# A four-batch, four-stage network on one core: the batch loop against four batches written out

## What is computed

```
x = u
x += gate * long_conv(mod(layernorm(x)))
x += gate * binary_ffn(mod(layernorm(x)))
x += gate * attention(mod(layernorm(x)))
x += gate * moe_top2(mod(layernorm(x)))
```

## Time and profile before

| | us |
|---|---|
| median of 3 executions | 2077.36 |
| lowest and highest | 2071.31, 2079.77 |
| the profiled execution's own time | 2071.98 |
| its span, first to last instruction | 2070.2 |
| around the span | 1.8 |
| mean granted clock of TensorE | 0.925 |
| busy: PE, DVE, ACT, POOL | 1795.0, 1520.4, 994.4, 735.9 |

### The profile page before, as it was taken

How to read it: one execution, slowest core, us unless ns; L and a number is a source line. 1 busy time by engine, 2 the same in 40 slices (tenths; PEclk the granted TensorE clock), 3 DMA queues, 4 the chain that set the end, 5 groups by cost and what they waited for, 6 DMA issues and landing times.

```text
span 2070.2 us, 27393 instructions
## 1 busy us (share of the span) xinstructions
PE 1795.0 (87%) x9108; PEld 1441.8 (70%) x9108; DVE 1520.4 (73%) x2758; ACT 994.4 (48%) x2129; POOL 735.9 (36%) x763
## 2 busy tenths in 40 slices
PE   6877789999875879999977779999987687999997
PEld 3755677777764757777765567777776575777786
DVE  4588878875659778887458887888564977788746
ACT  1313266777320347777431326677732033676743
POOL 0052245543225144454115224544321513455321
PEclk7888899999998989999989899999998897999998
DMA  6500244341410043543150024444141004344315
GB/s 231 203 1 1 77 123 119 98 104 42 188 53 1 1 122 98 139 118 73 29 223 0 1 62 135 112 107 103 43 187 54 1 1 122 98 118 123 78 27 203
DMA packets 92187, 187.17 MB, mean 90 GB/s; under 512 B 29119, under 2 KB 44287, under 8 KB 88326
## 3 DMA queue, kind: packets, MB, share of 16 engines
q1 hardware_dynamic: 84742, 171.66, 28.4%
q10 hardware_dynamic: 7296, 13.63, 2.3%
HBM read 129.39 MB, written 45.89 MB: 85 GB/s over the span
## 4 chain that ended last, share of the span: by engine, by line
PE 61%; DVE 17%; ACT 5%; DVEq 5%; issue 5%; POOL 3%; DMA 2%; ACTq 1%; SPq 1%; POOLq 0%
PE ps L389 8%; PE ps L512 7%; PE ps L532 6%; PE ps L534 6%; PE ps L555 5%; PE ps L552 5%; PE ps L553 5%; PE ps L684 5%; PE ps L395 5%; PE ps L725 3%; DMA gate_scratch<-grow 2%; DVE prod L1140 2%; PE ps L538 2%; DVE ps L1072 1%; DVE oT L1093 1%
## 5 line engine op out<-in xcount | busy, mean ns | idle before, releaser
L1072 DVE CUSTOM_DVE_ANT_0 ps<-ps,mrow 128x128 f32<-128x128 f32 (+7 forms) x512 | 385.2, 765 | 119.0 <-PE ps L512 117.1
L1305 POOL TENSOR_TENSOR psplit<-pT,psplit 128x384 fp32r<-128x384 f32 (+3 forms) x320 | 302.4, 958 | 429.9 <-ACT psplit L808 427.8
L808 ACT ACTIVATE psplit<-ps 128x512 fp32r<-128x512 f32 (+3 forms) x768 | 373.2, 486 | 0.0
L807 ACT ACTIVATE pT<-ps 128x512 f32<-128x512 f32 (+3 forms) x512 | 256.7, 501 | 169.8 <-PE ps L538 87.1
L512 PE MATMUL ps<-khl,qhh 128*128 128x512 f32 (+3 forms) x768 | 251.1, 391 | 36.5 <-DMA qhh<-work 16.5
L532 PE MATMUL ps<-qhh,khl 128*128 128x512 f32 (+3 forms) x768 | 271.9, 354 | 4.6 <-ACT psplit L808 4.1
L534 PE MATMUL ps<-q,k 65*128 65x512 f32 (+3 forms) x768 | 268.6, 350 | 0.0
L552 PE MATMUL ps<-psplit,vhi 128*65 128x512 f32 (+3 forms) x768 | 265.2, 345 | 0.0
L555 PE MATMUL ps<-psplit,vhi 128*65 128x512 f32 (+3 forms) x768 | 259.7, 338 | 0.0
L553 PE MATMUL ps<-psplit,vlo 128*65 128x512 f32 (+3 forms) x768 | 259.4, 338 | 0.0
L764 ACT ACTIVATE work<-ps,modb 128x512 f32<-128x512 f32 x48 | 37.4, 779 | 402.1 <-PE ps L467 402.1
(11 more groups left out here) (179 smaller groups left out, 3513.8 us busy)
## 6 DMA issues: line engine op xcount, KB each, us to landing
qhh<-q_scratch SPq DMA_DIRECT2D x112, 256.0 KB, 5.1
q_scratch<-hrow SPq DMA_DIRECT2D x24, 1024.0 KB, 7.0
mix<-inverse_scratch SPq DMA_DIRECT2D x64, 256.0 KB, 3.6
q<-q_scratch SPq DMA_DIRECT2D x56, 256.0 KB, 4.5
sgn<-sgn_scratch SPq DMA_DIRECT2D x8, 1024.0 KB, 13.7
Kf<-kf_scratch SPq DMA_DIRECT2D x4, 2048.0 KB, 17.5
khl<-k_scratch SPq DMA_DIRECT2D x24, 256.0 KB, 8.2
in_w<-in_w_scratch SPq DMA_DIRECT2D x4, 1536.0 KB, 10.9
```

The lines of the kernel that those rows point to most:

```text
L807: A(full(n)[:, 0:hi - lo], ps[:, b, 0:hi - lo], ACT.Exp, scale=SCALE)
L808: A(psplit[:, n % PRING, 0, 0:hi - lo], ps[:, b, 0:hi - lo], ACT.Exp, scale=SCALE)\
L1072: V.tensor_tensor_reduce(out=v, in0=v, in1=mrow[:, L - n:L], scale=1.0, scalar=-3e38, op0=ALU.add, op1=ALU.max, accum_out=mx[:, u % 2, i:i ...
L1305: G.tensor_tensor(psplit[:, n % PRING, 1, 0:m], full(n)[:, 0:m], psplit[:, n % PRING, 0, 0:m].bitcast(F32), ALU.subtract)\
```

## The change

The loops over the batches become Python loops, so the four passes are written out one behind the other, on all five engines. Semaphores are no longer cleared between batches. Instead each wait inside a batch asks for its count plus the batch's number times what that semaphore gains in a batch (table `EACH`, function `at`), and the numbers of the banks' semaphores go on counting. `part_ends` and the clearing stay once, between the setup and the first batch. PE alone gets two new waits at the start of a batch: for the last batch's low parts of `hT`, and for the seven loads. In the last batch the next batch's normalisation, its input load and the seven loads and the wait for them are left out.

```diff
+        now = {"batch": 0}
+        def at(name, n):
+            return s[name], n + now["batch"] * EACH.get(name, 0)
...
+        def begin(bi):
+            now["batch"] = banks["batch"].batch = bi
+            banks["batch"].at = 0
...
-            with pe.Fori(0, B):
-                bk.reset()
+            for bi in range(B):
+                begin(bi)
+                if bi:
+                    pe.wait_ge(*at("h_lo_done", 0))
+                    pe.wait_ge(*at("l0_loaded", 0))
...
-                for h in range(NHALF):
-                    normed(LN_NEXT, h)
+                if bi + 1 < B:
+                    for h in range(NHALF):
+                        normed(LN_NEXT, h)
...
-                part_ends(pe, "tensor")
...
-            with act.Fori(0, B):
-                act.wait_ge(s["tap_made"], 1)
+            for bi in range(B):
+                begin(bi)
+                act.wait_ge(*at("tap_made", 1))
...
-                for h in range(NHALF):
-                    normed(LN_NEXT, h, modn)
-                part_ends(act, "scalar")
+                if bi + 1 < B:
+                    for h in range(NHALF):
+                        normed(LN_NEXT, h, modn)
...
-                pick_first((bi + 1) % B)
-                dve.wait_ge(s["x_next_loaded"], 16)
-                dve.wait_ge(s["hT_done"], (LN_MOE + 1) * NHALF * ND)
-                for h in range(NHALF):
-                    stats(xn, range(4 * h, 4 * h + 4))
-                    normed(LN_NEXT, h, xn)
-                for h in range(NHALF):
-                    h_low(LN_NEXT, h)
+                if bi + 1 < B:
+                    pick_first(bi + 1)
...
                 dve.drain().then_inc(s["x_done"], 1)
-                part_ends(dve, "vector")
...
-                for h in range(NHALF):
-                    normed(LN_NEXT, h)
+                if bi + 1 < B:
+                    for h in range(NHALF):
+                        normed(LN_NEXT, h)
...
-                part_ends(pool, "gpsimd")
...
-            with sp.Fori(0, B) as bi:
-                sp.wait_ge(stored, 16)
-                sp.sem_clear(stored)
-                dma(x[:, :, :], d["x"][bass.ds(bi, 1), :, :].rearrange("a (t p) n -> p (a t) n", p=P))\
+            for bi in range(B):
+                begin(bi)
+                if bi:
+                    sp.wait_ge(stored, 16 * bi)
+                dma(x[:, :, :], d["x"][bi:bi + 1, :, :].rearrange("a (t p) n -> p (a t) n", p=P))\
                     .then_inc(s["x_loaded"], 16)
...
-                dma(xn[:, :, :], d["x"][bass.ds((bi + 1) % B, 1), :, :].rearrange("a (t p) n -> p (a t) n", p=P))\
-                    .then_inc(s["x_next_loaded"], 16)
+                if bi + 1 < B:
+                    dma(xn[:, :, :], d["x"][bi + 1:bi + 2, :, :].rearrange("a (t p) n -> p (a t) n", p=P))\
+                        .then_inc(s["x_next_loaded"], 16)
...
-                    dma(dst, src).then_inc(s["l0_loaded"], 16)
-                sp.wait_ge(s["l0_loaded"], 16 * 7)
-                sp.wait_ge(s["x_done"], 1)
+                        dma(dst, src).then_inc(s["l0_loaded"], 16)
+                    sp.wait_ge(*at("l0_loaded", 16 * 7))
+                sp.wait_ge(*at("x_done", 1))
...
-                clear()
-            sp.wait_ge(stored, 16)
+            sp.wait_ge(stored, 16 * B)
```

More of the change, by code:

```diff
@@ L335, in reset @@
             def reset(self):
-                self.low = 0
+                self.low, self.batch = 0, 0
                 self.at, self.uses, self.frees, self.owner, self.chunk = 0, [0] * 8, [0] * 8, [None] * 8, {}
@@ L381, in _ @@
         def _(pe):
+            begin(0)
             mm, tr = nc.tensor.matmul, nc.tensor.transpose
@@ L429, in _ @@
                     modulation(layer // 2)
-            pe.wait_ge(s["filter_sine"], 3)
+            pe.wait_ge(*at("filter_sine", 3))
             for t in range(0, NT, 2):
-                b = bk.take(pe, ("kern", t), until=(s["kern_done"], t // 2 + 1))
+                b = bk.take(pe, ("kern", t), until=at("kern_done", t // 2 + 1))
                 for u in range(2):
@@ L461, in normed @@
                 for dt in range(ND):
-                    b = bk.take(pe, ("ln", k, h, dt), until=(s["hT_done"], (k * NHALF + h) * ND + dt + 1))
+                    b = bk.take(pe, ("ln", k, h, dt), until=at("hT_done", (k * NHALF + h) * ND + dt + 1))
                     for u in range(4):
@@ L477, in h_ready @@
             def h_ready(k, h):
-                pe.wait_ge(s["h_lo_done"], (k * NHALF + h + 1) * ND)
+                pe.wait_ge(*at("h_lo_done", (k * NHALF + h + 1) * ND))
             def project(k, col):
                 for e in range(2):
-                    b = bk.take(pe, ("rope", k, e), until=(s["rope_a"], 2 * k + e + 1))
+                    b = bk.take(pe, ("rope", k, e), until=at("rope_a", 2 * k + e + 1))
                     h, c = k % 2 if k >= 4 else k // 2, col + e * P
@@ L490, in project_values @@
                 for t in range(4 * h, 4 * h + 4, 2):
-                    b = bk.take(pe, ("v", t), until=(s["v_copied"], t // 2 + 1))
+                    b = bk.take(pe, ("v", t), until=at("v_copied", t // 2 + 1))
                     for u in range(2):
@@ L516, in turn_maxima @@
             def turn_maxima(u):
-                b = bk.take(pe, ("nm", u), until=(s["nmr_done"], u + 1))
-                pe.wait_ge(s["nm_done"], u + 1)
+                b = bk.take(pe, ("nm", u), until=at("nmr_done", u + 1))
+                pe.wait_ge(*at("nm_done", u + 1))
                 tr(ps[0:NT, b, 0:P], nm[:, u % 2, :], ident[:, :]).then_inc(ready[b], 1)
@@ L524, in score_cols @@
                 lo, hi = max(c * HALF, j * P), (c + 1) * HALF
-                b = bk.take(pe, ("cols", u, c, j), until=(s["exp_done"], NBLK * u + 4 * c + j + 1))
+                b = bk.take(pe, ("cols", u, c, j), until=at("exp_done", NBLK * u + 4 * c + j + 1))
                 if c == 0 and j == 0:
                     if u == 0:
-                        pe.wait_ge(s["first_cols"], 16 * 4)
+                        pe.wait_ge(*at("first_cols", 16 * 4))
                     else:
@@ L557, in gated_rows @@
             def gated_rows(dt):
-                pe.wait_ge(s["vx_done"], dt + 1)
+                pe.wait_ge(*at("vx_done", dt + 1))
                 for h in range(NHALF):
-                    b = bk.take(pe, ("vrow", dt, h), until=(s["vrow_done"], dt * NHALF + h + 1), at=2 * dt + h)
+                    b = bk.take(pe, ("vrow", dt, h), until=at("vrow_done", dt * NHALF + h + 1), at=2 * dt + h)
                     for u in range(4):
@@ L569, in up_rows @@
                 for h in range(NHALF):
-                    b = bk.take(pe, ("up", n, h), until=(s["conv_done"], n + 1), at=(2 * n + 4 * (n // 4)) % 8 + h)
+                    b = bk.take(pe, ("up", n, h), until=at("conv_done", n + 1), at=(2 * n + 4 * (n // 4)) % 8 + h)
                     split_mm(ps[:, b, :], lambda a, q: in_w[:, a, q, e * P:(e + 1) * P],
@@ L636, in _ @@
                             normed(LN_FFN, 1)
-                        b = bk.take(pe, ("ffn1", h, n), until=(s["gelu_done"], h * NH1 + n + 1))
+                        b = bk.take(pe, ("ffn1", h, n), until=at("gelu_done", h * NH1 + n + 1))
                         sign_mm(ps[:, b, :], lambda a, q: sgn1[:, q, n * P:(n + 1) * P],
@@ L1322, in value_low @@
                                     ALU.subtract).then_inc(s["v_done"], 1)
-            with pool.Fori(0, B):
+            for bi in range(B):
+                begin(bi)
                 pool.drain().then_inc(s["tap_made"], 1)
                 for n, e in enumerate(E_ORDER):
-                    pool.wait_ge(s["tap_done"], NHALF * n + 1)
+                    pool.wait_ge(*at("tap_done", NHALF * n + 1))
                     v = tapped(e)[:, 0:2]
```

276 lines of the change are left out of this document (147 added, 129 removed), and 4 rows, old and new, of the table EACH.

## The result

The four batches written out take 2025.01 us (median of 4, 2021.88 to 2031.72) against 2078.57 us (four executions of the kernel before, one more than in its table): a ratio of 0.9755, with a 95% interval of 0.9724 to 0.9785. So it is faster by about 2.3%, some 45 to 54 us.

What follows compares the result with a forecast made beforehand. The prediction took PE to bound the kernel, with holes at the ends of passes and slow starts behind them. Gains of 26.4 + 7.9 + 5.4 = 39.7 us gave 2032.3 to 2037.7, named as 2035 us, range 2026 to 2045.

Steps and rivals of the forecast that it cites:

- The sum: Whole kernel: the gains at the ends of passes, from the clock and in the last batch add up to 39.7 us.
- The hole (26.4 us): Ends of passes 1 to 3: PE goes on at once without loop, meeting or clearing, gaining 3 x 8.8 = 26.4 us.
- The clock (7.9 us): Starts of batches 2 to 4: without a hole the first 24 products run like later ones, gaining 7.9 us.
- part 3: From the 24th product on, the path keeps its waits and only starts about 11.4 us earlier; cost nothing.
- rival B: Batch starts: PE goes on, but clock or first taps give part back; gain 25 to 34 us, chance 0.17.
- The last batch (5.4 us): Last batch: experts' second product starts without transposing a nonexistent batch's rows, 5.9 us, less 0.5 for POOL: 5.4 us.
- 0.5 us for POOL beside DVE's splits: Last batch: POOL's bias work moves beside DVE's splits and slows them; bounds 0 and 3 us, 0.5 taken.
- Table loads (0, with 0.5 us as a condition): ACT, batches 2 to 4: both loads go, worth 0; the first, if kept, would delay the first tap about 0.5 us.
- rival D: ACT's table loads were on the path: up to 9.0 us more gain, 2023 to 2029 us, chance 0.07.
- The store, the gates, the instructions: Batch ends and starts: PE needs no wait for the store, gates arrive in time, instructions come fast enough; cost nothing.
- Rivals A and C: A: hole is the store's, 2065 to 2071 us, chance 0.04; C: instructions come too slowly, about 2160 us, chance 0.02.
- The level (2035 us): Whole kernel: the middle between 2032.3 us from the profiled execution and 2037.7 us by the median.

Runs made afterwards that it cites:

- experiments 2 and 3: 2: changed kernel with the meeting and clearing back between batches, no branch: 2043.59 us, 0.9841. 3: kernel before storing only first 128 rows per batch: 2062.60 us.
- experiment 1: Both kernels run once more, unaltered: the changed kernel 2029.74 us, ratio 0.9784; the kernel before 1.0022 of itself.
- experiment 4: Changed kernel in which PE alone also waits at the start of a batch for the last batch's store: 2056.36 us, ratio 0.9894.
- experiment 7: Changed kernel with POOL's expert bias begun later: 2018.91 us, ratio 0.9735; repeated, 2014.03 us, 0.9709, beside the changed kernel's 2026.91 us, 0.9772.
- experiment 6: Changed kernel with an Exp, and so a table load, put in front of the first tap of batches 2 to 4: 2038.87 us in one execution.

## Why the prediction was right, and where not

**The sum: right, and in part by luck.** The mechanisms were those named, but the 38.0 us of the stages meet the forecast's 39.7 only because errors cancel: the clock gave 4.3 us less than forecast, the hole and the last batch together 2.6 more.

**The hole (26.4 us): right.** It is gone to the last, and PE waits for nothing in its place. The end of batches 1 to 3 shortened by 27.4 us in the mean. What it was made of, 6.3 us of branch and 2.5 us of meeting, is shown by experiments 2 and 3 and by the instruction packets; the forecast had priced it as a whole.

**The clock (7.9 us): the mechanism right, the size wrong.** The first 24 products gained 2.9 us in each batch (8.41 to 5.47), a little more than the 2.6 forecast. The step that failed is its silent half, that the products behind them would stay as they were: part 3 said that the rest of the path "keeps its waits and only starts about 11.4 us earlier". It keeps its waits, 0.6 and 1.8 us, but now they bring the clock down, and the second 24 take 7.2 to 7.4 us. In passes 2 to 4 of the kernel before they did so in two of six only. All twelve profiles, with four starts of a batch in each, tell when: I set the second 24 products against the 48 in front of them. Nine passes had 48 products of 13.69 us or more, all behind a hole, and there the second 24 took 5.7 to 5.8; the other 39 had 13.40 us or less, and there they took 7.2 to 8.6 (in six of the 39 the first of the two waits is longer, 0.7 to 1.4 us). Some of the 39 stand behind a hole too, such as the two of experiment 1 with 12.81 and 12.72. So what sorts them is not the hole: the clock stayed up through those waits where it had come up late, and fell where it had been up longer. This is the order that the profiles show, and experiment 4 could bring the late rise about; why the clock does so is not shown. A written-out batch, with 11.2 to 11.3 us for the 48, is always of the second kind. Where the kernel before had the fall too, the gain of the start was 25.2 - 23.5 = 1.7 us; where it had not, 24.5 - 23.5 = 1.0. Net 3.6 us for three batches. This is what rival B described, at a place that it had not named.

**The last batch (5.4 us): right, a little small**, 5.3 in the first profile and 7.0 in the mean. The step that it counted against the gain, 0.5 us for POOL beside DVE's splits, is half right: DVE's cast and difference are 2.0 us slower together, where the forecast had up to 3 us for four operations, but PE did not wait for them in any of the three profiles, and where experiment 7 takes POOL away nothing is gained there. Its cost is 0.

**Table loads (0, with 0.5 us as a condition): right** by experiment 6. Seven loads of 17 are gone, and rival D's 9.0 us are not: a load costs what of it lies on the path. The Trainium skill (ScalarE: Activation LUTs, section "What ACT_TABLE_LOAD costs") gives about 2.66 us a switch, and the estimate by it, 18.6 us for seven, does not come out here either.

**The store, the gates, the instructions: right.** POOL's gate terms ran without a wait for the gates, and PE's idle time put down to issue is 0.8 us in all, in the setup, as before. The written-out kernel doesn't fetch more either: the pages count 80 and 69 instruction packets on the two queues before, 74 and 64 after. Rivals A and C fall.

**The level (2035 us).** The three terms came to 38.0 us against 39.7. Yet the medians moved by 45 to 54 us. The forecast weighed one profiled execution of the kernel before. Its executions and the changed kernel's differ among themselves by 4.5 us of setup and up to 4 us of attention stage in a batch, as the clock falls or does not in short pauses. The two profiles of the kernel before are fast executions of it (2071.98 and 2068.47 us, against medians of 2078.57 and 2078.73), those of the changed kernel lie on both sides of its medians. The profiles' mean spans (2068.5 and 2025.0) are 43.4 us apart, of which 5.4 lie in the setup and in stages that the change doesn't touch. Whether the rest, some 5 us between the profiles' 43.4 and the medians' mean of 48 to 50, is chance or a clock that falls less often in a kernel with fewer pauses, stays open: no run told it apart.

## What to carry to other kernels

A loop over a long body costs more than its meeting: here 6.3 us behind every taken branch, the time to bring the loop's first instructions back, a third of it because a large store was just under way, and then a slow start of TensorE. Four passes can simply be written out. Before pricing a clock gain, follow the path to the next pauses: here 1.4 to 1.6 of the 2.9 us that a faster start gave were taken back in two short waits by a fall of the clock that the old, later rise had kept off. And where two engines slow each other, look at which of the two PE waits for; moving the other's work by some microseconds gave 4.5 us a batch here.

## What was not expected of the hardware

- The same setup code ends at about 90 or about 94 us, seven and five times in twelve profiles. PE's clock is what differs: 16 products of the filter (L434, L459) take 7.19 us in the five late ones and 3.72 to 4.20 in the seven others.
- The time behind a taken branch depends on what is being transferred: 6.2 to 6.3 us with a store of 1 MB just issued, 4.1 to 4.2 with 128 KB. The instruction packets come 3.3 us behind the clearing in the one and 1.1 us in the other.
- In one place a pause of 1.72 us was followed by the lower clock and one of 1.53 us was not. And the two waits of 0.6 and 1.8 us at the head of a batch (the first up to 1.4 in six passes) were followed by it in 39 passes and not in the nine in which the clock had come up late from a hole. So here a slow start of a stage kept off a slow middle.
